# Moving the rounding of the gated weights and the last layers' weight work into softmax attention

## What is computed

```python
x = x + _L0_xattn_ref(_layernorm(x), ctx, ctx)
x = x + _L0_ffn_ref(_layernorm(x), ...)
x = x + _L1_xattn_ref(_layernorm(x), ctx, ctx, ...)
x = x + _L1_ffn_ref(_layernorm(x), ...)
x = x + _L2_xattn_ref(_layernorm(x), ctx, Wq, bq, Wk, bk, Wv, bv, Wo, bo)   # softmax attention, 16 heads
x = x + _L2_ffn_ref(_layernorm(x), w_gate, w_up, w_down)                    # gated feed-forward
x = x + _L3_xattn_ref(_layernorm(x), ctx, decay, W_in, b_in, W_out, b_out, gamma, beta)
x = x + _L3_ffn_ref(_layernorm(x), kernel, bias)
```

```python
def weight_quant(w):
    scale = 1.0 / jnp.clip(jnp.mean(jnp.abs(w)), 1e-05, None)
    return jnp.clip(jnp.round(w * scale), -1, 1) / scale
```

## Time and profile before

| | us |
|---|---|
| median of three runs (1838.95 to 1842.91) | 1840.26 |
| the profiled execution, its own time | 1840.84 |
| its span in the trace | 1839.1 |

### The profile page before, as it was taken

One profiled execution on the slowest core, in us unless ns is written; L12 is line 12 of the kernel. 1 busy time (PEld: TensorE's weight loads), 2 busy tenths in 40 slices (PEclk: granted clock), 3 DMA queues, 4 the chain that ended last, 5 costly groups with the idle time before them and its releaser, 6 DMA issues. The chain is left out here.

```text
span 1839.1 us, 32255 instructions
## 1 busy us (share of the span) xinstructions
PE 1329.7 (72%) x11572; PEld 842.1 (46%) x11572; DVE 1318.3 (72%) x2817; ACT 1103.6 (60%) x1564; POOL 580.3 (32%) x1046
## 2 busy tenths in 40 slices
PE   4999999999899759885266674699998266772111
PEld 2565666565777525554023333366665224341110
DVE  5788888887555246788699997366665578765996
ACT  4588888877222147776378887244443268784564
POOL 6556666643200231110134331111110011114663
PEclk9799999999999879997556767799999578776555
DMA  7567777765200023330100000211110400000211
GB/s 224 158 175 180 182 188 183 179 156 112 51 0 0 5 65 79 75 78 18 50 1 1 1 1 1 64 33 39 34 38 12 120 1 1 0 1 23 58 35 46
DMA packets 97396, 122.64 MB, mean 67 GB/s; under 512 B 30064, under 2 KB 82488, under 8 KB 92252
## 3 DMA queue, kind: packets, MB, share of 16 engines
q1 hardware_dynamic: 97244, 120.66, 25.5%
HBM read 82.17 MB, written 24.98 MB: 58 GB/s over the span
## 5 line engine op out<-in xcount | busy, mean ns | idle before, releaser
L1018 DVE TENSOR_REDUCE ratt_nmax<-ratt_psS 128x2 f32<-128x512 f32 x512 | 318.6, 683 | 62.5 <-PE ratt_psS L777 62.0
L914 ACT ACTIVATE ratt_E<-ratt_psT 128x1024 f32<-128x1024 f32 x256 | 255.1, 1022 | 74.2 <-PE ratt_psT L795 74.0
L777 PE MATMUL ratt_psS<-ratt_K,ratt_Q 72*128 72x256 bf16 x1024 | 203.1, 282 | 7.8 <-DVE ratt_nmax L1018 3.1
L795 PE MATMUL ratt_psT<-ratt_Q,ratt_K 75*128 75x256 bf16 x1024 | 196.8, 275 | 1.9 <-DMA ratt_Q<-ratt_rows 1.6
L819 PE MATMUL ratt_psO<-ratt_E,ratt_V 128*32 128x256 f32 x2048 | 138.8, 389 | 0.3 <-ACT ratt_E L914 0.3
L777 PEld LDWEIGHTS ratt_psS<-ratt_K,ratt_Q 72*128 72x128 bf16 x1024 | 80.6, 99 | 97.6 <-DVE ratt_nmax L1018 61.8
L795 PEld LDWEIGHTS ratt_psT<-ratt_Q,ratt_K 75*128 75x128 bf16 x1024 | 100.2, 99 | 19.6 <-issue 2.1
L3597 PE MATMUL final_psT<-final_identh,final_Z 128*128 128x128 f16 x64 | 8.2, 310 | 111.0 <-ACT final_Z L3631 111.0
L2389 PE MATMUL nffn_psH<-nffn_W,nffn_QT 128*128 128x512 bf16 x128 | 55.8, 586 | 31.5 <-ACT nffn_H L2468 20.3
L819 PEld LDWEIGHTS ratt_psO<-ratt_E,ratt_V 128*32 128x32 f32 x2048 | 53.8, 110 | 50.5 <-issue 27.7
L2589 POOL TENSOR_TENSOR all_X<-all_X,satt_bo 128x1024 f32<-128x1024 f32 x8 | 18.9, 2364 | 168.2 <-DVE all_X L2655 168.2
(11 more groups left out here) (468 smaller groups left out, 3702.1 us busy)
## 6 DMA issues: line engine op xcount, KB each, us to landing
ratt_K<-context_parts SPq DMA_DIRECT2D x96, 192.0 KB
ratt_Q<-z_parts SPq DMA_DIRECT2D x32, 576.0 KB
gatt_V<-in_ctx_dram SPq DMA_DIRECT2D x16, 512.0 KB, 6.6
context_parts<-ratt_CS SPq DMA_DIRECT2D x48, 128.0 KB, 6.5
z_parts<-ratt_ZS SPq DMA_DIRECT2D x48, 128.0 KB, 4.8
head_sums<-ratt_O SPq DMA_DIRECT2D x64, 72.0 KB
all_X<-in_x_dram SPq DMA_DIRECT2D x16, 256.0 KB, 4.0
ratt_C<-in_ctx_dram SPq DMA_DIRECT2D x16, 256.0 KB, 4.0
```

The lines of the kernel that those rows point to most:

```text
L777: mm = nc.tensor.matmul(psS[:, RING[h], c * D:(c + 1) * D], Q9[0:R, buf, h, n % 2, c * P:(c + 1) * P], K9[0:R, buf, h, n % 2, :], start=Tr ...
L795: mm = nc.tensor.matmul(psT[:, j % 2, e, c, :], K9[0:RM, buf, h, u, c * P:(c + 1) * P], Q9[0:RM, buf, h, u, :], start=True, stop=True)
L914: sc.activation(E[:, m % 2 * 2 + p // 2, 2 * (p % 2):2 * (p % 2) + 2], psT[:, j % 2], ACT.Exp, scale=SCALE).then_inc(exped, 1)
L1018: v.tensor_reduce(nmax[:, n % 2, h, :], psS[:, RING[h]].rearrange("p (c t) -> p c t", c=2), AX.X, ALU.max, negate=True).then_inc(maxed, 1)
```

## The change

`late_setups` goes, with its block and its barrier (an unused function, `ternary`, goes too). Its work is spread over three places.

- The last layers' weights (`LastWeights`) are loaded by SP in step 0 of softmax attention, after the first load of the context. PE turns the three squares at position 2 and makes the products at position 5, ahead of the first scores; DVE rounds at position 2 and finishes at position 5, ahead of the first maximum. The results use PSUM banks of the attention (`heads.psS`, `psO`, `psP`, `psF`). SP stores the summaries in step 1 and reloads them in step 2.
- The three gated matrices (`GatedWeights`) are loaded by SP in step 2, after waits for all of the above (they use the same SBUF as the last layers' tiles). ACT sums the absolute values at three positions in steps 2 and 3. The sum over the partitions is no longer a matmul: SP stores the row sums to DRAM in step 4 and reads them back spread over all partitions in step 5, and DVE reduces them. DVE rounds in nine slots in steps 5 to 8, one instruction in each.
- The 48 transposes on PE and the six copies on ACT stand at the head of the feed-forward's block, into that block's own PSUM banks; the first product waits for all six copies.

The diff, cut to its core:

```diff
+class GatedWeights:
+    SLOTS = {(5, 4): 0, (5, 5): 1, (6, 0): 2, (6, 4): 3, (6, 5): 4, (7, 0): 5, (7, 4): 6, (7, 5): 7, (8, 0): 8}
+    ABS = {(2, 4): 0, (3, 3): 1, (3, 4): 2}
...
+    def row_sum(self, act, g, i):
+        if (g, i) in self.ABS:
+            m = self.ABS[g, i]
+            act.wait_ge(self.w_in, 16 * self.M)
+            self.nc.scalar.activation(self.R[:, m], self.W[:, m], ACT.Abs,
+                                      accum_out=self.rowsum[:, m:m + 1]).then_inc(self.summed, 1)
+    def scales(self, dve):
+        v = self.nc.vector
+        dve.wait_ge(self.rows_in, 16)
+        v.tensor_reduce(self.total[:], self.rows[:].rearrange("p q m -> p m q"), AX.X, ALU.add).then_inc(
+            self.totals, 1)
...
+    def round(self, dve, g, i):
+        if (g, i) == (5, 0):
+            self.scales(dve)
+        if (g, i) in self.SLOTS:
...
+            elif n % 3 > 0:
+                dve.wait_ge(self.steps, n)
+            if n % 3 == 0:
+                v.tensor_scalar(W, W, self.inv[:, m:m + 1], MAGIC, ALU.mult, ALU.add).then_inc(self.steps, 1)
+            elif n % 3 == 1:
+                v.tensor_scalar(W, W, MAGIC, 1.0, ALU.subtract, ALU.min).then_inc(self.steps, 1)
+            else:
+                v.tensor_scalar(self.R[:, m], W, -1.0, None, ALU.max).then_inc(self.steps, 1)
+class LastWeights:
...
+    def leave(self, sp):
+        sp.wait_ge(self.k_steps, self.KSTEPS)
+        sp.wait_ge(self.summed_up, 1)
+        sp.wait_ge(self.back_turned, 1)
+        sp.wait_ge(self.late_in, 32)
+        sp.wait_ge(self.sum_out, 16)
+        for g in range(2):
+            self.late.load_summaries(self.nc, sp, self.sums, g)
...
+    def finish(self, dve):
+        v, step, bs, late = self.nc.vector, self.step, self.bs, self.late
+        dve.wait_ge(self.summary_steps, 1)
+        dve.wait_ge(self.hid, KC)
...
@@ softmax_attention, SP
                     sp.wait_ge(v_used, vs)
                     sp.dma_start(CG[:], CT[:, :, bass.ds(at, G * P)]).then_inc(c_in, 16)
+                    if g == 0:
+                        last.load(sp)
+                    if g == 2:
+                        last.leave(sp)
+                        gated.load(sp)
+                    if g == 5:
+                        gated.load_rows(sp)
                     sp.wait_ge(taken, ks)
                     heads.expand(sp, g, lambda rows, half: KT[rows, :, half * HG:(half + 1) * HG], free)
+                    if g == 1:
+                        last.store(sp)
+                    if g == 4:
+                        gated.store_sums(sp)
@@ softmax_attention, DVE
                         if is_group(bg) and 1 <= i < G:
                             max_and_shift(bg, i)
+                        if g == 0 and i == G + 1:
+                            last.finish(dve)
                         if is_group(g) and i == G + 1:
                             max_and_shift(g, 0)
...
+                        if g == 0 and i == 2:
+                            last.round(dve)
+                        gated.round(dve, g, i)
@@ softmax_attention, PE
+                        if g == 0 and i == G + 1:
+                            last.products(pe)
...
+                        if bg == 0 and i == 1:
+                            last.taken(pe)
...
                                 project(g, 1, WK, CG)
+                                if g == 0:
+                                    last.turn(pe)
@@ softmax_attention, ACT
+                            if g == 0:
+                                last.copy(act)
                         if is_group(bg) and 1 <= i < G:
                             exp(bg, i)
+                        gated.row_sum(act, g, i)
                         if is_group(g) and i == G + 1:
                             exp(g, 0)
@@ gated_ffn
-        late_setups(nc, io, ident, identb, [(io["L2_ffn_w_gate"], WG, ug), (io["L2_ffn_w_up"], WU, uu),
-                                            (io["L2_ffn_w_down"], W2, u2)], late, ST, wsum, sums)
@@ gated_ffn, PE
+                for m in range(weights.M):
+                    turn_weights(m)
                 pe.wait_ge(ident_set, 1)
                 turn_z(0)
+                pe.wait_ge(w_taken, 2 * weights.M)
                 first(0, 0)
@@ gated_ffn, ACT
+                for m in range(weights.M):
+                    take_weights(m)
                 act.wait_ge(ready, 5)
                 copy_z(0)
```

## The result

The changed kernel took 1816.8 us in the median of four runs (1816.19 to 1817.57), beside 1839.85 us for the kernel before on the same chip: a ratio of 0.9879, 95% interval 0.9863 to 0.9896. The forecast was 1819.0 us in a range of 1809.5 to 1826.5, and faster. The profiled execution took 1816.19 us; the forecast for it was 1819.6.

What follows compares the result with a forecast made beforehand. No engine bounds the whole; PE bounds attention. Stage -34.1, head clock -1.0, step 0 +1.5, two runs +3.4, last run +8.7, row sums +0.3 make -21.2 us: 1819.0 us, range 1809.5 to 1826.5.

Steps and rivals of the forecast that it cites:

- the stage: Between attention and feed-forward: the whole setups stretch goes, barrier included, -34.1 us.
- clock in the feed-forward's head: Feed-forward's head: transposes keep PE at work, so group 0's turning and first half products run faster; -1.0 us (0 to -2.2).
- step 0: Attention's step 0: the last layers' work on DVE makes the first maximum late; +1.5 us, between 0.5 and 6.0.
- two runs of rounding: Steps 5 to 7: three DVE rounding instructions per run delay subtractions PE needs; 1.7 us each, +3.4 us.
- last run: Rounding reaching step 8, without projections to hide under: 4.5 us late plus 4.2 us of fallen clock, +8.7 us (2.2 to 11).
- row sums and loads: ACT's row sums in steps 2 and 3 and SP's loads cost nothing, or 0.3 us if one sum runs over.
- The scales: Step 5: a DVE reduction and two small operations fit before the exponential; cost nothing, or 1 us.
- no fall of the clock: Rival, last step: PE's clock stays up, all else as forecast without 4.2 us; -25.4, 1815 us; chance 0.18.
- DVE and POOL don't meet: Rival, rounding: POOL's addition doesn't block it; a run costs 0.77 us, the last 2.2; -29.6, 1810.7 us; chance 0.15.
- upper bound of 6.0: Rival, step 0: clock falls in pauses before and after the first scores; +4.5 us on the forecast, 1823.5 us; chance 0.10.
- late copy of weights: Rival, feed-forward's head: the first product waits for the weights' copies; +2 us, 1821 us; chance 0.06.
- lowered clock in steps 5 to 7: Rival: DVE's lateness there makes PE pause long enough for 1.2 GHz; slower than before, some 1848 us; chance 0.03.

Runs made afterwards that it cites:

- the other order: Kernels that, against the changed kernel, round the bias at position 1 of step 0 and add the hidden term at position 4; alone 1820.5 us.
- the warm head: Changed kernel plus 32 unread PE transposes ahead of group 0 in the feed-forward's head; 1816.5 us, ratio 0.9883 to the kernel before.
- changed again: The changed kernel run once more without any edit, as yardstick; 1817.1 us, ratio 0.9890 to the kernel before.
- order of step 0: Changed kernel with, in step 0, the bias rounded at position 1 and the hidden term's additions at position 4; 1820.5 us, ratio 0.9907 to the kernel before.

## Why the prediction was right

By its own terms, against the profiled execution of the changed kernel:

| term | forecast | measured |
|---|---|---|
| the stage | -34.1 | -33.94 |
| clock in the feed-forward's head | -1.0 | 0 |
| step 0 | +1.5 | +1.55 |
| two runs of rounding | +3.4 | +2.28 |
| last run | +8.7 | +5.32 |
| row sums and loads | +0.3 | 0 |
| elsewhere (start of attention -1.11, feed-forward +0.98, final +0.1) | 0 | 0.0 |
| sum | -21.2 | -24.8 |

- **The stage.** Right: nothing of the setups was needed, the block starts 1.06 us after attention.
- **The head.** The weights' transposes and copies are hidden: the sixth copy ends at 1442.17, 6.7 us after the start, as worked out, and ACT takes up group 0 9.52 us after the start, before 9.53. The clock term failed. PE's pause ahead of group 0 was 3.81 us where I had 2.6, and I took "PE keeps busy" for "the clock is up in the products"; it rose at about 1439, fell in the 3.81 us of PE's pause, and even where it was held through the pause it fell at the products.
- **Step 0.** The sum came out, and for most of its steps: PE pauses 2.54 us ahead of its bias product as forecast. The first maximum is at 1186.79; forecast was 1187.5 for an attention that starts 1.11 us later, that is 1186.4. But I expected 2.4 GHz there, and the scores still took 1.97 us at a granted clock of 0.54 (from 1184.75 to 1186.75), nearly as in the earlier trace rows. In the five traces with 28.8 to 28.9 us the first scores did take 1.09 us; there the clock fell behind the next pause (2.39 us) instead, and the step cost 0.5 us more, not less. The experiments show the clock's place to be free: between the spreads, the changed order of this step took 28.3 to 28.9 us, and the other order 26.0 to 27.7. The agreement to 0.05 us is luck.
- **The loads.** The three matrices were issued at 1219.90 to 1221.17, and the last one landed 13.3 us later, at 1234.5, where I had 1230 to 1232 from the 10.7 us of the earlier trace rows. The keys' spread of step 2 started on time all the same (30.40 us after step 1's).
- **Two runs of rounding.** The mechanism was right row by row (PE's waits, POOL's 3.21, DVE's 3.27); the size was 1.14 us a run and not 1.7. Without POOL a run costs 0.65 (forecast 0.77), POOL adds 0.49 (forecast 0.9). DVE's instructions that don't wait for each other start some 0.08 us before the earlier one's recorded end (1.28 us from 1338.14, the next at 1339.34), which I had not taken off. With POOL, the second instruction started 0.16 us sooner in the step than I had it (1342.13, that is 1250.54 in the times of the earlier trace rows), and it, POOL's addition and the third together took 4.52 us (1342.13 to 1346.65) in place of 4.83: the subtraction ended 0.47 us earlier than forecast.
- **The last run.** Mis-sized, and the largest error: 5.32 in place of 8.7. Lateness was 3.87 us (forecast 4.5, for the same reason), the clock cost 1.45 (forecast 4.2). I foresaw one pause of 3.6 us with 0.50 behind it. In two further traces it was there (3.16 us), with 1.94 and 5.3 us lost; in the first trace, and in that of the warm head, the clock had already fallen in the pause before, which hid half of the second pause and cost less. The forecast 8.7 lies inside what the traces of the same schedule give, 5.3 to 9.15.
- **The rest.** Attention's start (-1.11) and the feed-forward (+0.98) cancel. Both lie inside what the traces differ by without an edit there, so this is luck too.
- **The scales.** They cost nothing. The first small operation on them took 1.45 us beside POOL's addition, and DVE's next work had time.

Of the rivals, "no fall of the clock" is ruled out by every trace of the changed schedule, though the time it gives, 1815, is nearer to the measured 1816.8 than the forecast is, because the clock's cost was at its small end and each run of rounding cost less than forecast. "DVE and POOL don't meet" is ruled out by the 3.27 and 3.21 us, and step 0 cost at most 2.1 us between the spreads in any trace, far from its upper bound of 6.0. There was no late copy of weights, and no lowered clock in steps 5 to 7 (1.00 from step 5's spread to step 7's). The feed-forward's +0.98 can't be put down to the change: it took 204.6 to 211.3 us in the experiments, with the same instructions in all but the two kernels with the warm head.

## What to carry to other kernels

Work that is put beside a bound engine costs by its place in the queue of its own engine and not by its length: the same nine instructions cost 7.6 us where they stand ahead of a subtraction that PE waits for and beside POOL's long addition, and nothing two or three positions earlier, where DVE stands idle anyway. Look in the timeline for idle time in square brackets that a PE result ends, take it only if it is longer than the instruction, and keep DVE's long SBUF instructions away from POOL's. And at the end of a pipeline, where the bound engine has nothing else to do, count each wait in full, and give the clock behind it a term with a range of its own; 24 transposes on PE whose results nobody reads held it in the two traces that had them.

## What the runs showed of the hardware that I had not expected

- The granted clock fell to 0.50 after PE pauses of only 1.46 us, while in the earlier trace rows it stood at 1.00 through 2.5 us of standing. The same instructions of step 8 with the same pause of 1.46 us kept 1.00 in two other traces (changed again, order of step 0), and in the one without POOL's addition. So where it falls isn't settled by the one pause in front of it. A loss of 1.45, 1.94 or 5.3 us followed from the same instructions. The two traces in which it fell there, the first and that of the warm head, agree within 0.02 us from attention's head (20.03 and 20.05) to its end (47.22 and 47.21); what sets the one course or the other stays open.
- The clock fell at the start of the feed-forward's first products (0.54 over 3 us in which PE was busy for 2.89), after a stretch at 0.97 whose last 4 us had PE busy for only 0.7.
- A DVE instruction on three columns, `gated_units`, took 1.45 us beside a POOL addition, where such small ones take 0.15 to 0.2; POOL's addition, which had started first, wasn't lengthened (2.38 us):

```profile
1311.33 2.38 POOL L2737 TENSOR_TENSOR all_X<-all_X,satt_bo 128x1024 f32<-128x1024 f32 x1 [20.09 <-DVE all_X L2805]
1311.55 0.70 DVE L2493 TENSOR_REDUCE satt_total<-satt_rows 128x3 f32<-128x384 f32 x1 [0.36 <-DMA satt_rows<-row_sums]
...
1312.28 1.45 DVE L2496 TENSOR_SCALAR gated_units<-satt_total 128x3 f32<-128x3 f32 x1
```

The reduction between them ran beside POOL without a delay that can be seen (0.70 us for 384 columns); only the `tensor_scalar` waited, until 1313.7, when POOL's addition ended.
